# Attention with 16 heads on Trainium2: the softmax division is moved from the probabilities to the attended output

## The chip, the cores and the metric

One core of a Trainium2 chip runs one program. The metric is the device time of the whole program in microseconds (us), lower is better. The engines named below are PE (the matrix engine, with PEld for its weight loads), ACT (scalar engine), DVE (vector engine), POOL (GpSimd), and SP, which issues the DMAs. PSUM has eight banks of 128 x 512 fp32.

## The reference

Two transformer-like blocks follow each other on x of shape (32, 128, 512): 32 sequences of 128 tokens, 512 features. The change touches only the attention of the first block:

```
h   = gamma * layernorm(x) + beta              # gamma, beta from cond, per sequence
qkv = h @ Wqkv.T + bqkv                        # 16 heads of 32
energy = einsum('bhqd,bhkd->bhqk', q, k)
att = softmax(energy, axis=-1) / 512 ** 0.5
out = einsum('bhqk,bhkd->bhqd', att, v)
h1  = out @ Wp.T + bp + x
x1  = gamma * layernorm(h1) + beta + h1
```

The second block (one attention over 512 features, then an MLP of 2048) reads x1.

## The kernel before, in words

The program has three stages. Stage A computes the first block, stage B the attention of the second, stage C its MLP. One tile is one sequence of 128 tokens (t = 0 to 31). Only stage A is changed.

Large products (keys, queries, values, the output projection) are done in fp32r with the operands split into a high and a low half: `split_product` issues three matmuls of 512 columns for each of four slices of the contraction, so each such block has 12 matmuls (lines 547 to 549). Keys and queries are computed for a group of four sequences at a time, one quarter of them in each iteration, a group ahead; so the last four iterations (t = 28 to 31) have none. The normalised input of tile t + 8 is transposed in iteration t (`norm_a`, line 571), so the iterations from t = 24 on have none. Values of tile t + 1 are computed in iteration t; iteration 31 has none.

The order of the matrix engine in an iteration t is written out by hand, and each engine works through its own list in order, waiting on semaphores:

- PE: scores(t) into four banks (32 instructions, line 619), values(t+1), keys, transposes of the probabilities for j = 0 and 1 (`transpose_p`, line 626, four each), queries, transposes for j = 2 and 3, `norm_a(t+8)`, project(t-1), attend(t) (line 637, 32 instructions).
- ACT: `exps(t, j)` for j = 0 to 3 (line 1030): four exponentials each, with the row sums as accumulated output; after j = 1, `round_o(t-1)` (line 1038), which copies the attended output out of its bank; then `copy_k`, and `scale_a` and `round_a` for tile t + 8.
- DVE: the four negated row maxima (line 1290), four reciprocals of the sums (line 1313), `copy_v` (line 1297), `low_o(t-1)` (line 1318), the statistics of two layer norms, four copies of the transposed probabilities (`copy_pt`, line 1308), `norm2`, `copy_q`, `add_x1`, and `residual(t-1)` (line 1328), which reads the projection's bank.
- POOL: the bias of the residual input, `scale_p(t, j)` for j = 0 to 3 (line 1662), which multiplies the 128 x 512 exponentials by the reciprocals, `shift(t-2)`, `norm_a(t+9)`.

So each group of exponentials goes ACT, DVE (reciprocal), POOL (multiplication), PE (transpose). `j` numbers the four banks of scores: bank j holds the heads m * 4 + j. The factor 512 ** -0.5 is applied in `round_o` and `low_o`.

Of the kernel before, what the change touches and what calls it, by code (L numbers as in the profile page):

```python
# [11 lines left out]
P = 128  # L12
# [66 lines left out]
def block_pair_kernel(nc, xt, cond_t, cols_d, bp0_d, bv0_d, pb1_d, b2_d, wg_t, wb_t, wqkv, wp0,  # L79
                      film1, film2, wq1_t, wk1_t, wv1_t, wp1, w1, w2, out):  # L80
    with ExitStack() as ctx:
# [84 lines left out]
        pa = run("pa", [P, HM, C, P])  # L166
        pta = run("pta", [P, HM, C, P])
        o_hi = run("o_hi", [P, 2, C, P], F32R)
# [113 lines left out]
        rec_ready, p_scaled = sem("rec_ready"), sem("p_scaled")  # L282
        o_hi_ready, o_lo_ready = sem("o_hi_ready"), sem("o_lo_ready")
# [58 lines left out]
        def h_full(n):  # L342

            if n < GB:
                return (hf[:, 0], hf[:, 1], pa[:, 2], pa[:, 3])[n]
            return hf[:, n % 2]
# [197 lines left out]
        def _(pe):  # L544
# [78 lines left out]
            def transpose_p(t, j):  # L623
                pe.wait_ge(p_scaled, HM * t + j + 1)
                for m in range(C):
                    last = nc.tensor.transpose(scores_bank[j][:, m * P:(m + 1) * P], pa[:, j, m, :], ident[:])
                last.then_inc(tp_done, 1)

            def attend(t):

                pe.wait_ge(v_copied, t + 1)
                wait(pe, o_lo_ready, t)
                pe.wait_ge(pt_copied, HM * (t + 1))
                for m in range(C):
                    for j in range(HM):
                        f = (m * HM + j) * HD
                        last = nc.tensor.matmul(o_bank[j * HD:(j + 1) * HD, m * P:(m + 1) * P], va[:, t % 2, f:f + HD],
                                                pta[:, j, m, :], start=True, stop=True)
                last.then_inc(pv_done, 1)

# [44 lines left out]
            for t in range(NB):  # L685
                g, b = t // GB, t % GB
                ahead = g + 1 < NG
                scores(t)
                if t + 1 < NB:

                    if t == 0:
                        pe.wait_ge(q_copied, GB)
                    elif (t - 1) // GB + 1 < NG:
                        pe.wait_ge(q_copied, GB + t)
                    else:
                        pe.wait_ge(v_copied, t + 1)
                    values(t + 1)
                if ahead:
                    if b == 0:
                        pe.wait_ge(hi_ready, GB * (g + 2))  # L700
                        pe.wait_ge(lo_ready, GB * (g + 2))

                    if t < 2:
                        pe.wait_ge(k_copied, GB + t)
                    else:
                        pe.wait_ge(h1_ready, t - 1)
                    keys(g + 1, b)
                transpose_p(t, 0)
                transpose_p(t, 1)
                if ahead:  # L710
                    pe.wait_ge(v_copied, t + 2)
                    queries(g + 1, b)
                transpose_p(t, 2)
                transpose_p(t, 3)
                if t + AHEAD < NB:

                    pe.wait_ge(n_scaled_act, t + AHEAD - 2)
                    norm_a(t + AHEAD, x_bank)
                if t > 0:
                    if t == 1:  # L720
                        pe.wait_ge(wa_hi_made, 4)
                        pe.wait_ge(wa_lo_made, 6)

                    if ahead:
                        pe.wait_ge(k_copied, GB + t + 1)
                    else:
                        pe.wait_ge(h1_ready, t - 1)
                    project(t - 1)
                attend(t)


# [43 lines left out]
            pe.wait_ge(n_scaled_act, NB - 2)  # L775
# [198 lines left out]
        def _(act):  # L974
# [49 lines left out]
            def exps(t, j):  # L1024

                act.wait_ge(max_done, HM * t + j + 1)
                wait(act, tp_done, HM * (t - 1) + j + 1)
                for m in range(C):
                    h = j * C + m
                    last = nc.scalar.activation(pa[:, j, m, :], scores_bank[j][:, m * P:(m + 1) * P], ACT.Exp,  # L1030
                                                bias=neg_max[:, j * C + m:j * C + m + 1],
                                                accum_out=sums[:, t % 2, h:h + 1])
                last.then_inc(exp_done, 1)

            def round_o(t):
                act.wait_ge(pv_done, t + 1)
                wait(act, proj_done, t - 1)
                nc.scalar.activation(o_hi[:, t % 2].rearrange("p c t -> p (c t)"), o_bank[:], ACT.Copy, scale=INV_SQRT_D)\
                    .then_inc(o_hi_ready, 1)
# [8 lines left out]
            for t in range(NB):  # L1048
                g, b = t // GB, t % GB
                exps(t, 0)  # L1050
                exps(t, 1)
# [3 lines left out]
                exps(t, 3)  # L1055
                if g + 1 < NG:
                    copy_k(g + 1, b)
                if t + AHEAD < NB:
                    scale_a(t + AHEAD, x_bank)
                    round_a(t + AHEAD)  # L1060
            round_o(NB - 1)
# [133 lines left out]
        def _(dve):  # L1195
# [114 lines left out]
            def recip(t, j):  # L1310

                dve.wait_ge(exp_done, HM * t + j + 1)
                nc.vector.reciprocal(rec[:, j * C:(j + 1) * C], sums[:, t % 2, j * C:(j + 1) * C]).then_inc(rec_ready, 1)  # L1313

            def low_o(t):
                dve.wait_ge(o_hi_ready, t + 1)
                wait(dve, proj_done, t - 1)
                nc.vector.scalar_tensor_tensor(o_lo[:, t % 2].rearrange("p c t -> p (c t)"), o_bank[:], INV_SQRT_D,
                                               o_hi[:, t % 2].rearrange("p c t -> p (c t)").bitcast(F32),
                                               ALU.mult, ALU.subtract).then_inc(o_lo_ready, 1)  # L1320
# [47 lines left out]
            for t in range(NB):  # L1368
# [6 lines left out]
                recip(t, 0)  # L1375
                row_max(t, 3)
                recip(t, 1)
                if t + 1 < NB:
                    copy_v(t + 1)
                if t > 0:  # L1380
                    low_o(t - 1)
                recip(t, 2)
# [12 lines left out]
                recip(t, 3)  # L1395
                copy_pt(t, 0)
# [6 lines left out]
                copy_pt(t, 3)  # L1403
                if t > 1:
# [3 lines left out]

            var_2(NB - 2)
# [207 lines left out]
        def _(pool):  # L1617
# [41 lines left out]
            def scale_p(t, j):  # L1659

                pool.wait_ge(rec_ready, HM * t + j + 1)
                nc.gpsimd.tensor_tensor(pa[:, j], pa[:, j],  # L1662
                                        rec[:, j * C:(j + 1) * C].unsqueeze(2).broadcast_to([P, C, P]), ALU.mult)\
                    .then_inc(p_scaled, 1)

            for t in range(NB):
                add_bias(t, t % 2, xra, bp0, xr_in[t % 2], loaded(t // 2 + 1), xr_ready)
                for j in range(HM):
                    scale_p(t, j)
                if t > 1:  # L1670
                    shift(t - 2)
                if t + AHEAD + 1 < NB:
                    norm_a(t + AHEAD + 1)
# [110 lines left out]
```

## Time and profile before

| | us |
|---|---|
| runs of the kernel before | 1577.86, 1580.72, 1580.98 (median 1580.72) |
| the profiled execution, its time | 1577.86 |
| the profiled execution, its span | 1576.1 |
| first scores of stage A start | 54.8 |
| last attend of stage A ends, about | 547.9 |
| PE, PEld busy over the span | 1531.9 (97%), 1239.2 (79%) |
| DVE, ACT, POOL busy over the span | 780.5 (50%), 596.9 (38%), 578.9 (37%) |

The span runs from the first to the last instruction; the profiled execution took 1.8 us more than its span. A row of a timeline gives the start and the length in us, the engine, the line, the operation, the tiles (written <- read), the number of merged instructions, and in brackets how long the engine had been idle and who released it. Matmuls overlap each other, so the length of a matmul's row is longer than the time for which it keeps the next one off; that time is the distance between two starts.

### The profile page before, as it was taken

The page shows a single profiled execution, that of the slowest core. Times are in us where ns is not written, and L with a number is a line of the kernel's source. Part 1 is how long each engine was busy: PE and PEld are TensorE (multiplying, and loading weights), DVE is VectorE, ACT ScalarE, POOL GpSimd, SP SyncE. Part 2 cuts the span into 40 slices and gives each one's busy share as a digit, 9 for nine tenths or more (in the row PEclk, how much of TensorE's full clock was granted, in tenths as well). Part 3 has the DMA queues.
Part 4 walks back from the last instruction along what each step waited for, and adds up shares of the span by engine and source line. Part 5 has one row for each costly group of instructions (what it writes and reads, how often), then busy time and mean ns, then how long its engine had stood idle before and what let it go on. Part 6 is the DMA issues. An engine that isn't in the chain of part 4 may idle for free. (4 is left out here: it accounts for less than half of the span.)

```text
span 1576.1 us, 25094 instructions
## 1 busy us (share of the span) xinstructions
PE 1531.9 (97%) x8988; PEld 1239.2 (79%) x8988; DVE 780.5 (50%) x1613; ACT 596.9 (38%) x1883; POOL 578.9 (37%) x504
## 2 busy tenths in 40 slices
PE   5999999999998799999999999999999999999999
PEld 3888888888886547777777888888888888888887
DVE  5677777777766645444445524242423324252422
ACT  3655555555534335445556312121211212121210
POOL 5566676767545423444433302121110202121100
PEclk9999999999998899999999999999999999999999
DMA  7122223122214332232224402020100102010100
GB/s 252 55 87 75 94 75 102 68 101 68 75 66 176 128 134 101 102 106 80 80 87 160 154 1 74 7 69 11 67 13 24 55 0 73 7 67 13 53 0 28
DMA packets 56577, 117.72 MB, mean 75 GB/s; under 512 B 6288, under 2 KB 6288, under 8 KB 55984
## 3 DMA queue, kind: packets, MB, share of 16 engines
q1 hardware_dynamic: 56496, 116.65, 21.6%
q8 instruction: 49, 0.80, 0.2%
q14 instruction: 32, 0.26, 0.1%
HBM read 91.33 MB, written 25.30 MB: 74 GB/s over the span
## 5 line engine op out<-in xcount | busy, mean ns | idle before, releaser
L1183 ACT ACTIVATE gf<-bank,cols 128x512 f32<-128x512 f32 x128 | 88.2, 689 | 512.5 <-PE bank L549 512.5
L1599 DVE CAST g_hi<-gf 128x512 fp32r<-128x512 f32 x128 | 68.7, 537 | 427.6 <-ACT gf L1183 427.6
L1030 ACT ACTIVATE pa<-bank,neg_max 128x128 f32<-128x128 f32 x512 | 181.3, 408 | 144.0 <-DVE neg_max L1290 144.0
L547 PE MATMUL bank<-w_hi,g_hi 128*128 128x512 f32 x512 | 200.5, 392 | 0.0
L547 PE MATMUL bank<-hb_hi,w_hi 128*128 128x512 f32 x512 | 199.4, 389 | 0.6 <-issue 0.6
L549 PE MATMUL bank<-w_hi,g_lo 128*128 128x512 f32 x512 | 199.4, 389 | 0.0
L548 PE MATMUL bank<-w_lo,g_hi 128*128 128x512 f32 x512 | 199.2, 389 | 0.0
L549 PE MATMUL bank<-hb_hi,w_lo 128*128 128x512 f32 x512 | 199.2, 389 | 0.0
L548 PE MATMUL bank<-hb_lo,w_hi 128*128 128x512 f32 x512 | 199.2, 389 | 0.0
L1649 POOL TENSOR_TENSOR xrc<-xrc,b 128x512 f32<-128x512 f32 x32 | 48.3, 1536 | 301.8 <-DMA xrc<-x_dram 301.8
L1662 POOL TENSOR_TENSOR pa<-pa,rec 128x512 f32<-128x512 f32 x128 | 132.1, 1040 | 50.8 <-DVE rec L1313 50.8
L1682 POOL TENSOR_TENSOR rstd<-ve,neg_half 128x1 f32<-128x1 f32 x64 | 39.0, 610 | 296.0 <-DVE ve L1420 296.0
L1030 ACT ACTIVATION_READ_ACCUMULATOR pa<-bank,neg_max 128x1 f32 x512 | 127.2, 248 | 0.0
L547 PEld LDWEIGHTS bank<-hb_hi,w_hi 128*128 128x128 f32 x512 | 96.1, 188 | 21.0 <-issue 1.0
L549 PEld LDWEIGHTS bank<-w_hi,g_lo 128*128 128x128 f32 x512 | 96.1, 188 | 20.1
L548 PEld LDWEIGHTS bank<-hb_lo,w_hi 128*128 128x128 f32 x512 | 96.1, 188 | 19.9
L549 PEld LDWEIGHTS bank<-hb_hi,w_lo 128*128 128x128 f32 x512 | 96.1, 188 | 19.9
L548 PEld LDWEIGHTS bank<-w_lo,g_hi 128*128 128x128 f32 x512 | 96.2, 188 | 19.6
L547 PEld LDWEIGHTS bank<-w_hi,g_hi 128*128 128x128 f32 x512 | 96.1, 188 | 19.5
L1685 POOL TENSOR_SCALAR xnb<-xb,rstd 128x512 f32<-128x512 f32 x64 | 104.0, 1625 | 11.8 <-issue 7.0
L1290 DVE TENSOR_REDUCE neg_max<-bank 128x4 f32<-128x512 f32 x128 | 83.6, 679 | 46.3 <-PE bank L619 46.3
L1206 DVE TENSOR_TENSOR g_lo<-gf,g_hi 128x512 fp32r<-128x512 f32 x128 | 96.4, 753 | 4.4
(194 smaller groups left out, 3158.4 us busy)
## 6 DMA issues: line engine op xcount, KB each, us to landing
rows<-st_dram SPq DMA_DIRECT2D x32, 512.0 KB, 4.2
xb<-x_dram SPq DMA_DIRECT2D x64, 256.0 KB, 2.9
xa<-xt_in SPq DMA_DIRECT2D x32, 256.0 KB, 4.4
xra<-xt_in SPq DMA_DIRECT2D x32, 256.0 KB, 2.7
x_dram<-h SPq DMA_DIRECT2D x32, 256.0 KB, 2.0
xrb<-x_dram SPq DMA_DIRECT2D x32, 256.0 KB, 3.6
x_dram<-xrb SPq DMA_DIRECT2D x32, 256.0 KB, 2.0
xrc<-x_dram SPq DMA_DIRECT2D x32, 256.0 KB, 3.6
```

What stands on the lines that cost most here:

```text
L547: nc.tensor.matmul(dst, w_hi, a_hi, start=start, stop=False)
L548: nc.tensor.matmul(dst, w_hi, a_lo, start=False, stop=False)
L549: return nc.tensor.matmul(dst, w_lo, a_hi, start=False, stop=stop)
L1030: last = nc.scalar.activation(pa[:, j, m, :], scores_bank[j][:, m * P:(m + 1) * P], ACT.Exp, bias=neg_max[:, j * C + m:j * C + m + 1], acc ...
L1183: nc.scalar.activation(gf[f % 2][:], bank[f % 2][:], ACT.Gelu, bias=cols[:, B1_COL + f:B1_COL + f + 1])\
L1206: return nc.vector.tensor_tensor(dst, whole, high.bitcast(F32), ALU.subtract)
L1290: nc.vector.tensor_reduce(neg_max[:, j * C:(j + 1) * C], scores_bank[j][:].rearrange("p (h k) -> p h k", h=C), AX.X, ALU.max, negate=True) ...
L1599: nc.vector.tensor_copy(g_hi[:, r, :], gf[f % 2][:]).then_inc(g_hi_ready, 1)
L1649: nc.gpsimd.tensor_tensor(x[:, i], x[:, i], row[:], ALU.add).then_inc(ready, 1)
L1662: nc.gpsimd.tensor_tensor(pa[:, j], pa[:, j], rec[:, j * C:(j + 1) * C].unsqueeze(2).broadcast_to([P, C, P]), ALU.mult)\
L1682: nc.gpsimd.tensor_tensor(rstd1[:, i:i + 1], ve1[:, i:i + 1], neg_half[:, 0:1], ALU.pow).then_inc(rr, 1)
L1685: nc.gpsimd.tensor_scalar(xn[:, slot], x[:, i], rstd1[:, i:i + 1], None, ALU.mult).then_inc(ready, 1)
```

## The change

The exponentials are no longer divided before they are transposed. They go from ACT straight to the transposes, the attended output is multiplied by the reciprocals instead, and POOL's `scale_p` is gone. The attended output lies transposed (features on partitions, queries along the bank), so the reciprocals must be transposed too: DVE takes one reciprocal of all 16 sums, copies it spread over 32 columns a head into `recx` (128 x 512), PE transposes that in four instructions into `x_bank` (`recip_t`), ACT copies it with the factor 512 ** -0.5 into `rs` (`copy_r`), and DVE multiplies the attended output by it into `of` (`scale_o`). `round_o` and `low_o` then read `of`. `pa` has two slots in place of four. PE's order changes: the transposes for j = 0 come before the keys, `norm_a` comes before the transposes for j = 2 and 3, and `recip_t(t-1)` comes after scores(t). ACT's `copy_k` comes before `exps(t, 3)`; POOL's three remaining items are in another order.

```diff
             def transpose_p(t, j):
-                pe.wait_ge(p_scaled, HM * t + j + 1)
+                pe.wait_ge(exp_done, HM * t + j + 1)
                 for m in range(C):
-                    last = nc.tensor.transpose(scores_bank[j][:, m * P:(m + 1) * P], pa[:, j, m, :], ident[:])
+                    last = nc.tensor.transpose(scores_bank[j][:, m * P:(m + 1) * P], pa[:, j % 2, m, :], ident[:])
...
             def attend(t):
                 pe.wait_ge(v_copied, t + 1)
-                wait(pe, o_lo_ready, t)
+                wait(pe, o_scaled, t)
...
+            def recip_t(t):
+                if t + AHEAD < NB:
+                    pe.wait_ge(n_scaled_act, t + AHEAD - 1)
+                else:
+                    pe.wait_ge(r_copied, t)
+                pe.wait_ge(rec_ready, t + 1)
+                flat = recx[:].rearrange("p h d -> p (h d)")
+                for m in range(C):
+                    last = nc.tensor.transpose(x_bank[:, m * P:(m + 1) * P], flat[:, m * P:(m + 1) * P], ident[:])
+                last.then_inc(r_done, 1)
...
                 scores(t)
+                if t > 0:
+                    recip_t(t - 1)
...
                     values(t + 1)
+                transpose_p(t, 0)
...
                     keys(g + 1, b)
-                transpose_p(t, 0)
                 transpose_p(t, 1)
                 if ahead:
                     pe.wait_ge(v_copied, t + 2)
                     queries(g + 1, b)
+                if t + AHEAD < NB:
+                    if t == 0:
+                        pe.wait_ge(n_scaled_act, AHEAD - 2)
+                    else:
+                        pe.wait_ge(r_copied, t)
+                    norm_a(t + AHEAD, x_bank)
                 transpose_p(t, 2)
                 transpose_p(t, 3)
-                if t + AHEAD < NB:
-                    pe.wait_ge(n_scaled_act, t + AHEAD - 2)
-                    norm_a(t + AHEAD, x_bank)
...
+            recip_t(NB - 1)
...
             def exps(t, j):
                 act.wait_ge(max_done, HM * t + j + 1)
-                wait(act, tp_done, HM * (t - 1) + j + 1)
+                wait(act, tp_done, HM * t + j - 1)
...
+            def copy_r(t):
+                act.wait_ge(r_done, t + 1)
+                wait(act, o_scaled, t)
+                nc.scalar.activation(rs[:], x_bank[:], ACT.Copy, scale=INV_SQRT_D).then_inc(r_copied, 1)
+
             def round_o(t):
-                act.wait_ge(pv_done, t + 1)
+                act.wait_ge(o_scaled, t + 1)
                 wait(act, proj_done, t - 1)
-                nc.scalar.activation(o_hi[:, t % 2].rearrange("p c t -> p (c t)"), o_bank[:], ACT.Copy, scale=INV_SQRT_D)\
-                    .then_inc(o_hi_ready, 1)
+                nc.scalar.activation(o_hi[:, t % 2], of[:], ACT.Identity).then_inc(o_hi_ready, 1)
...
                 exps(t, 0)
+                if t > 0:
+                    copy_r(t - 1)
                 exps(t, 1)
                 if t > 0:
                     round_o(t - 1)
                 exps(t, 2)
-                exps(t, 3)
                 if g + 1 < NG:
                     copy_k(g + 1, b)
+                exps(t, 3)
...
+            copy_r(NB - 1)
             round_o(NB - 1)
...
-            def recip(t, j):
-                dve.wait_ge(exp_done, HM * t + j + 1)
-                nc.vector.reciprocal(rec[:, j * C:(j + 1) * C], sums[:, t % 2, j * C:(j + 1) * C]).then_inc(rec_ready, 1)
+            def recip(t):
+                wait(dve, r_done, t)
+                dve.wait_ge(exp_done, HM * (t + 1))
+                nc.vector.reciprocal(rec[:], sums[:, t % 2, :]).then_inc(rec_made, 1)
+                dve.wait_ge(rec_made, t + 1)
+                nc.vector.tensor_copy(recx[:], rec[:].unsqueeze(2).broadcast_to([P, HEADS, HD]))\
+                    .then_inc(rec_ready, 1)
+
+            def scale_o(t):
+                dve.wait_ge(r_copied, t + 1)
+                wait(dve, o_lo_ready, t)
+                dve.wait_ge(pv_done, t + 1)
+                nc.vector.tensor_tensor(of[:].rearrange("p c t -> p (c t)"), o_bank[:], rs[:], ALU.mult)\
+                    .then_inc(o_scaled, 1)
 
             def low_o(t):
                 dve.wait_ge(o_hi_ready, t + 1)
                 wait(dve, proj_done, t - 1)
-                nc.vector.scalar_tensor_tensor(...)
+                low_half(o_lo[:, t % 2], of[:], o_hi[:, t % 2]).then_inc(o_lo_ready, 1)
...
-                recip(t, 0)
                 row_max(t, 3)
-                recip(t, 1)
                 if t + 1 < NB:
                     copy_v(t + 1)
+                copy_pt(t, 0)
                 if t > 0:
-                    low_o(t - 1)
-                recip(t, 2)
+                    scale_o(t - 1)
...
-                recip(t, 3)
-                copy_pt(t, 0)
+                if t > 0:
+                    low_o(t - 1)
                 copy_pt(t, 1)
...
                 copy_pt(t, 3)
+                recip(t)
...
+            scale_o(NB - 1)
...
-            def scale_p(t, j):
-                pool.wait_ge(rec_ready, HM * t + j + 1)
-                nc.gpsimd.tensor_tensor(pa[:, j], pa[:, j],
-                                        rec[:, j * C:(j + 1) * C].unsqueeze(2).broadcast_to([P, C, P]), ALU.mult)\
-                    .then_inc(p_scaled, 1)
-
             for t in range(NB):
-                add_bias(t, t % 2, xra, bp0, xr_in[t % 2], loaded(t // 2 + 1), xr_ready)
-                for j in range(HM):
-                    scale_p(t, j)
+                if t + AHEAD + 1 < NB:
+                    norm_a(t + AHEAD + 1)
                 if t > 1:
                     shift(t - 2)
-                if t + AHEAD + 1 < NB:
-                    norm_a(t + AHEAD + 1)
+                add_bias(t, t % 2, xra, bp0, xr_in[t % 2], loaded(t // 2 + 1), xr_ready)
```

In the first group of tiles `h_full` uses `of` and `rs` in place of two slots of `pa`, and a later transpose into `x_bank` waits for the last `copy_r`. Stages B and C are unchanged.

## Rows read from the trace of the kernel before

**Rows 1.** The page: busy time, share of the span, instructions by engine.

```profile
PE 1531.9 (97%) x8988; PEld 1239.2 (79%) x8988; DVE 780.5 (50%) x1613; ACT 596.9 (38%) x1883; POOL 578.9 (37%) x504
```

**Rows 2.** Windows: length, each engine's busy us and count, clock, DMA, GB/s.

```profile
200.00:300.00 100.00, 100.00 (x832) 82.80 (x831) 75.20 (x164) 56.94 (x246) 69.55 (x60) 1.00 0.24 80
...
486.00:502.20 16.20, 13.26 (x116) 9.80 (x106) 9.78 (x20) 6.18 (x33) 7.19 (x7) 0.79 0.90 324
502.20:517.10 14.90, 11.75 (x108) 8.79 (x104) 9.77 (x20) 6.18 (x33) 7.20 (x7) 0.89 0.22 73
517.10:533.00 15.90, 12.96 (x108) 9.70 (x104) 9.78 (x20) 6.18 (x33) 7.18 (x7) 0.79 0.20 68
533.00:547.90 14.90, 9.89 (x96) 7.35 (x92) 9.44 (x20) 6.17 (x33) 7.16 (x7) 0.77 0.65 230
```

**Rows 3.** Timeline of PE, iteration t = 2: first instruction of each block.

```profile
83.90 1.17 PE L619 MATMUL bank<-ka,qa 32*128 32x128 f32 x32
85.00 0.50 PE L547 MATMUL bank<-wv_hi,h_hi 128*128 128x512 f32 x1
...
87.89 0.39 PE L547 MATMUL bank<-h_hi,wk_hi 128*128 128x512 f32 x1
...
90.62 1.03 PE L626 MATMUL bank<-ident,pa 128*128 128x128 f32 x8
91.41 0.48 PE L547 MATMUL bank<-h_hi,wq_hi 128*128 128x512 f32 x1
...
94.25 1.03 PE L626 MATMUL bank<-ident,pa 128*128 128x128 f32 x8
...
99.43 1.17 PE L619 MATMUL bank<-ka,qa 32*128 32x128 f32 x32
```

**Rows 4.** Timeline of PE: scores of t = 23, 24 and 25.

```profile
410.33 1.17 PE L619 MATMUL bank<-ka,qa 32*128 32x128 f32 x32
...
425.86 1.17 PE L619 MATMUL bank<-ka,qa 32*128 32x128 f32 x32
...
440.92 1.17 PE L619 MATMUL bank<-ka,qa 32*128 32x128 f32 x32
```

**Rows 5.** Timeline of PE ahead of the loop: four transposes between two product blocks.

```profile
45.54 0.60 PE L571 MATMUL bank<-ident,xa 128*128 128x128 f32 x4
45.90 0.48 PE L547 MATMUL bank<-h_hi,wk_hi 128*128 128x512 f32 x1
```

**Rows 6.** Waits, 55 to 550 us: total us, times, longest.

```profile
DVE h L1328 <- PE bank L549: 46.9, 31, 2.8
...
PE bank L626 <- POOL pa L1662: 14.0, 16, 3.7
```

**Rows 7.** Groups by line: busy us, mean ns of one, idle time before.

```profile
L1328 DVE TENSOR_TENSOR h<-bank,xra 128x512 f32<-128x512 f32 x32 | 22.1, 692 | 47.6 <-PE bank L549 47.6
```

**Rows 8.** Timelines of PE, DVE and ACT, iteration t = 13.

```profile
255.00 1.17 PE L619 MATMUL bank<-ka,qa 32*128 32x128 f32 x32
...
256.24 1.29 DVE L1290 TENSOR_REDUCE neg_max<-bank 128x4 f32<-128x512 f32 x2 [1.45 <-PE bank L619]
...
256.96 0.37 ACT L1030 ACTIVATE pa<-bank,neg_max 128x128 f32<-128x128 f32 x1 [3.42 <-DVE neg_max L1290]
...
259.72 0.64 ACT L1038 ACTIVATE o_hi<-bank 128x512 fp32r<-128x512 f32 x1
260.20 0.41 ACT L1030 ACTIVATE pa<-bank,neg_max 128x128 f32<-128x128 f32 x1
...
262.94 0.78 ACT L1022 ACTIVATE ka<-bank,cols 128x512 f32<-128x512 f32 x1
```

**Rows 9.** Timeline of PE, iteration t = 29, without keys and queries.

```profile
502.19 1.17 PE L619 MATMUL bank<-ka,qa 32*128 32x128 f32 x32
...
511.73 1.12 PE L626 MATMUL bank<-ident,pa 128*128 128x128 f32 x4 [0.45 <-POOL pa L1662]
512.49 0.78 PE L547 MATMUL bank<-wp_hi,o_hi 128*128 128x512 f32 x1
```

More of the change, by code:

```diff
@@ L165, in block_pair_kernel @@
         pa_at = run.offset
-        pa = run("pa", [P, HM, C, P])
+        pa = run("pa", [P, 2, C, P])
         pta = run("pta", [P, HM, C, P])
+        recx = run("recx", [P, HEADS, HD])
+        rs = run("rs", [P, D])
+        of = run("of", [P, C, P])
         o_hi = run("o_hi", [P, 2, C, P], F32R)
@@ L281, in block_pair_kernel @@
         tp_done, pt_copied, pv_done = sem("tp_done"), sem("pt_copied"), sem("pv_done")
-        rec_ready, p_scaled = sem("rec_ready"), sem("p_scaled")
-        o_hi_ready, o_lo_ready = sem("o_hi_ready"), sem("o_lo_ready")
+        rec_made, rec_ready, r_done, r_copied = sem("rec_made"), sem("rec_ready"), sem("r_done"), sem("r_copied")
+        o_scaled, o_hi_ready, o_lo_ready = sem("o_scaled"), sem("o_hi_ready"), sem("o_lo_ready")
         proj_done, xr_ready, h1_ready = sem("proj_done"), sem("xr_ready"), sem("h1_ready")
@@ L344, in h_full @@
             if n < GB:
-                return (hf[:, 0], hf[:, 1], pa[:, 2], pa[:, 3])[n]
+                return (hf[:, 0], hf[:, 1], of[:], rs[:].rearrange("p (c t) -> p c t", c=C))[n]
             return hf[:, n % 2]
@@ L774, in _ @@
             pe.wait_ge(film_copied, 2)
-            pe.wait_ge(n_scaled_act, NB - 2)
+            pe.wait_ge(r_copied, NB)
             for c in range(C):
@@ L1026, in exps @@
                 act.wait_ge(max_done, HM * t + j + 1)
-                wait(act, tp_done, HM * (t - 1) + j + 1)
+                wait(act, tp_done, HM * t + j - 1)
                 for m in range(C):
-                    h = j * C + m
-                    last = nc.scalar.activation(pa[:, j, m, :], scores_bank[j][:, m * P:(m + 1) * P], ACT.Exp,
+                    h = m * HM + j
+                    last = nc.scalar.activation(pa[:, j % 2, m, :], scores_bank[j][:, m * P:(m + 1) * P], ACT.Exp,
                                                 bias=neg_max[:, j * C + m:j * C + m + 1],
@@ L1317, in low_o @@
                 wait(dve, proj_done, t - 1)
-                nc.vector.scalar_tensor_tensor(o_lo[:, t % 2].rearrange("p c t -> p (c t)"), o_bank[:], INV_SQRT_D,
-                                               o_hi[:, t % 2].rearrange("p c t -> p (c t)").bitcast(F32),
-                                               ALU.mult, ALU.subtract).then_inc(o_lo_ready, 1)
+                low_half(o_lo[:, t % 2], of[:], o_hi[:, t % 2]).then_inc(o_lo_ready, 1)
             def residual(t):
```

## Prediction, on record before the change was run

> **What bounds the kernel now.** I read four views in this order: the page's busy shares, windows over stage A, PE's timeline inside one iteration, and the waits.
>
> The page has PE at 97% of the span and nothing else above 50% [rows 1]. Since a matmul's row is longer than the time it keeps its successor off, this alone doesn't prove that PE is the limit. The windows tell the stages of the loop apart. Between 200 and 300 us PE is busy 100.00 of 100 us at clock 1.00, while DVE has 75, POOL 70 and ACT 57 [rows 2]. In the last four iterations PE is busy 13.26 of 16.2, 11.75 of 14.9, 12.96 of 15.9 and 9.89 of 14.9, and the mean clock is 0.77 to 0.89, so part of each runs at 1.2 GHz and not at 2.4 [rows 2]: there a chain through the other engines sets the pace. The proof that PE is the limit in the first 28 is in the periods. Iteration 23 takes 425.86 - 410.33 = 15.53 us, as does t = 2 (99.43 - 83.90), and iteration 24, which differs for PE by four missing transposes, takes 440.92 - 425.86 = 15.06 [rows 3, 4]. Take work from PE and the iteration shrinks by 0.47 us at once; work added there should lengthen it. PE waits for POOL only where keys and queries are missing: the 16 waits sum to 14.0 us [rows 6], four blocks of transposes in each of four iterations.
>
> So `scale_p`, the work removed, blocks PE in 4 of 32 iterations, and the work added to PE lies in all of them.
>
> **The change, part by part.** The sum is made for the profiled execution, 1577.86 us (span 1576.1 plus 1.8); the median of the runs shown is 1580.72, 2.9 above it.
>
> *Removed.* POOL loses four multiplications an iteration and DVE four small reciprocals. In the loop's first 28 iterations nothing on PE waits for them, so this is worth nothing there.
>
> *`recip_t` on PE.* Four transposes in iterations 1 to 27. The price as a distance between starts has two bounds. Ahead of the loop, four lone transposes take 45.90 - 45.54 = 0.36 us until the next product starts [rows 5]. Values take 87.89 - 85.00 = 2.89 us when they follow scores, queries 94.25 - 91.41 = 2.84 when they follow transposes, keys 90.62 - 87.89 = 2.73 when they follow another product [rows 3]; with `recip_t` in between, values follow transposes and take 0.05 less. That gives 0.31 as the lower bound. The upper is the 0.47 by which iteration 23 exceeds 24. I take the middle, 0.39; times 27 that is 10.5 us.
>
> *The moved transposes.* A run of eight is split: values, four, keys, four, queries. Now eight take 91.41 - 90.62 = 0.79 and the queries behind them 0.11 more than keys behind values: 0.90. Split, it is 2 x (0.36 + 0.11) = 0.94. That is 0.04 more; the rows are rounded to 0.01, so between 0.02 and 0.06, and 28 x 0.03 = 0.8 us. `norm_a` stays in a run of twelve transposes: nothing.
>
> *Does anything make PE wait in these iterations?* Time 0 is the start of scores; distances between starts are from [rows 8] and [rows 3]. PE: scores to 1.1, `recip_t` to 1.5, values to 4.3, j = 0 to 4.7, keys to 7.5, j = 1 to 7.9, queries to 10.7, norm to 11.1, j = 2 to 11.5, j = 3 to 11.9, project to 14.8, attend to 15.9. DVE's first maximum starts 256.24 - 255.00 = 1.24 after the scores' start, which is 0.14 after their end, and two maxima last 1.29, so 0.6 each; ACT's first exponential starts at 1.96. A group of four exponentials takes (259.72 - 256.96) / 2 = 1.38, `round_o` 0.48 (260.20 - 259.72), `copy_k` 0.78; `copy_r`, also a 128 x 512 ACT copy out of PSUM, gets `round_o`'s 0.48. So exps 0 ends at 3.3, `copy_r` at 3.8, exps 1 at 5.2. `scale_o` is the step with a new wait. It stands behind `copy_v` (values end at 4.3, released 0.14 later like the maxima) and `copy_pt(0)`; with the 0.6 of a maximum for each it starts at 5.7 and, at the 0.69 of the nearest row (a DVE product-bank read with an SBUF operand [rows 7]), ends at 6.4. `round_o` ends at 6.9, exps 2 at 8.3, `copy_k` at 9.1, exps 3 at 10.5 to 10.7. PE wants it at 11.5. Slack: 0.8 us. Behind ACT's wait for `scale_o` stand exps 2 and 3, and for them wait the transposes for j = 2 and 3, `copy_pt` and attend, so this is the chain that matters. `low_o` ends near 8.6 and project needs it at 11.9. The last `copy_pt` ends near 12.9 and attend needs it at 14.8. The reciprocal and its spread copy have no row of their size; nothing at the least, at the most 0.69 each [rows 7], they end by 14.3; `recip_t` wants them at 17.0. `residual` waits for project until 15 anyway: DVE has waited there 46.9 us in 31 times, 1.5 each [rows 6]. POOL's list is shorter by four 128 x 512 multiplications. SP's loads and stores wait for the same events, in the same order. I cost all of this at nothing; the cover is PE itself, and where it goes by d us in every iteration, the price is 28 d.
>
> *The last four iterations.* Now j = 3 starts at 511.73 - 502.19 = 9.54 after the scores and project at 10.3 [rows 9]. In the new order values end at 4.3, `scale_o` at 6.4, `round_o` at 6.9, exps 2 at 8.3, exps 3 at 9.7, so j = 3 starts near 9.8. What lay between exps 3 and j = 3 (9.54 - 1.96 - 4 x 1.38 - 0.48 = 1.6) is gone, but `copy_r` (0.48) and the wait for `scale_o` (ACT finished exps 1 at 5.2 and stands until 6.4) take its place. That is 0.25 later in each of three iterations, 0.8 us. Iteration 31 has no values, so `copy_pt(0)` and `scale_o` come earlier: exps 3 ends near 8.7, against 9.54 now: 0.8 us less. `recip_t(31)` adds 0.4. Together +0.4. The time at 1.2 GHz will be about what it is, since the idle time ahead of project is: now 9.54 less 4.0 of scores and values and 1.1 of three transposes, 4.4 us; then 0.6, 2.7 and 1.0, 4.3 us. Its bounds are the two rivals on these four below.
>
> Sum: 10.5 + 0.8 + 0.4 = 11.7 us, 1577.9 + 11.7 = 1589.6 for an execution like the profiled one and 1592.4 for one at the median. I say 1591.
>
> PE's busy share leaves a question. The Trainium skill (Perfetto Trace Analysis, "Identifying the Most-Contended Engine") calls matmul busy time a bad measure of headroom and wants the weight-load share read. That share is 82.80 of 100 us here [rows 2], which would leave 17 us in 100, and the new transposes would cost nothing: 1579. The periods of iterations 23 and 24 speak against it.
>
> The Trainium skill (TensorE: Matmul & The Clock Gate, "Part 4: PE-mode transpose") has about 275 ns for a transpose in a kernel. Taken as a price that makes an estimate of 1.1 us for four, 34 us for 31 times, and 1612. The row of eight here lasts 1.03 us but holds the queries off for 0.79 [rows 3], so durations overlap and the distance counts.
>
> **The rivals.**
>
> *A stall behind `scale_o`.* If DVE reaches `scale_o` or finishes it over 0.8 us later than I reckon, j = 3 starts late in every iteration. For it: DVE exchanges four small operations for a spread copy and a product of 128 x 512, and ACT now waits in the middle of its exponentials. Against it: each step has a row. At 0.5 us late in 28 iterations it adds 14: 1605. It decides from 0.8 us of slip.
>
> *The last four iterations gain.* If the clock stays full there, they take 9.8 + 0.4 + 2.9 + 1.0 = 14.1 three times and 13.0 once, 55.7 with `recip_t(31)`, against 61.9 in the windows [rows 2]: 6.2 less, so 11.3 - 6.2 = 5.1 in total, 1583 or 1586 at the median. For it: `values`, `recip_t` and j = 0 now run without a break. Against it: PE still idles about 4 us before project.
>
> *PE has room.* The transposes hide in gaps between matmuls. Then nothing moves by more than 1 us: 1580. Against it: the 0.47 us.
>
> *Faster: the POOL hop was the whole limit of the last four.* If they ran at PE's own length, about 10 us each, 61.9 would fall to 40 and the total by 22 - 11.3 = 11: 1567 to 1570. It decides when these four give back more than 11.3, 2.8 each. Against it: sixteen exponentials take 5.5 us from 1.96 on, and project and attend (4) stand behind them, which no order here shortens below 11.5.
>
> **How the numbers follow.** Forecast 66% (1587 to 1596), stall 13% (to 1610), gain in the last four 12%, PE has room 5%, faster 4%. The range 1584 to 1602 leaves out the last two and most of the deep stall. A difference of 0.2%, about 3 us, is what a measurement of this kernel tells from none. The forecast, the stall and the gain are slower by more; of the rest about 6% lies within it: slower 0.90, within 0.06, faster 0.04.
>
> **What would show it.** Right: scores of full iterations 15.9 to 16.0 us apart, PE still busy 100 of 100; the four transposes of `recx` hold the values off by 0.36 to 0.44; no wait of PE behind exponentials before t = 28; the last four together within 2 us of 61.9. Wrong: PE idle before j = 2 or 3 in the full iterations, with `scale_o` at its root; or the four transposes costing under 0.2; or a clock of 1.00 in the last four.

## The result and the profile after

The changed kernel takes 1592.88 us (median of 4 runs, 1591.71 to 1594.01), the kernel before 1579.29 in the same series (4 runs, 1577.75 to 1580.98). The ratio is 1.0086, with a 95% interval of 1.0068 to 1.0103: slower by 0.9%. The profiled execution took 1592.22 us with a span of 1590.4, 14.3 more than the span before; the forecast was 11.7 more.

The page of the changed kernel, busy time by engine, answers to [rows 1]:

```profile
PE 1544.8 (97%) x9116; PEld 1250.8 (79%) x9116; DVE 829.0 (52%) x1581; ACT 616.8 (39%) x1915; POOL 461.1 (29%) x376
```

POOL gave up 118 us of work, PE gained 128 instructions, DVE 49 us. The span went with PE. PE's share is 97% as before, and the windows show why that is no sign of standing still. They answer to [rows 2]; the last window is a piece of iteration 31.

```profile
200.00:300.00 100.00, 100.00 (x838) 82.48 (x838) 85.16 (x155) 60.58 (x256) 43.32 (x32) 1.00 0.24 80
...
547.00:557.20 10.20, 7.50 (x24) 5.63 (x25) 7.03 (x14) 5.34 (x27) 3.44 (x3) 0.51 0.55 220
```

In the middle of the loop PE is busy 100.00 of 100 us, as it was, while POOL fell from 70 to 43 us and DVE rose from 75 to 85. The second window matters further down: in 10.2 us of the last iteration the clock was almost all the time 1.2 GHz (0.51 of full).

One full iteration (t = 12) on PE, first instruction of each group, answers to [rows 3]:

```profile
242.21 1.17 PE L622 MATMUL bank<-ka,qa 32*128 32x128 f32 x32
243.31 0.66 PE L653 MATMUL bank<-ident,recx 128*128 128x128 f32 x4
243.72 0.47 PE L550 MATMUL bank<-wv_hi,h_hi 128*128 128x512 f32 x1
...
246.58 0.60 PE L629 MATMUL bank<-ident,pa 128*128 128x128 f32 x4
246.93 0.48 PE L550 MATMUL bank<-h_hi,wk_hi 128*128 128x512 f32 x1
...
249.79 0.60 PE L629 MATMUL bank<-ident,pa 128*128 128x128 f32 x4
250.14 0.48 PE L550 MATMUL bank<-h_hi,wq_hi 128*128 128x512 f32 x1
...
252.98 0.60 PE L574 MATMUL bank<-ident,xa 128*128 128x128 f32 x4
253.42 1.04 PE L629 MATMUL bank<-ident,pa 128*128 128x128 f32 x8
254.21 0.48 PE L550 MATMUL bank<-wp_hi,o_hi 128*128 128x512 f32 x1
...
257.16 1.08 PE L640 MATMUL bank<-pta,va 128*32 128x128 f32 x32
258.17 0.39 PE L622 MATMUL bank<-ka,qa 32*128 32x128 f32 x4
```

The reader should see that no row has an idle time in brackets, and that the starts follow the forecast's list: scores to 1.1, `recip_t` to 1.5, values to 4.4, the end at 258.17 - 242.21 = 15.96 us. The four transposes of `recx` keep the values off by 243.72 - 243.31 = 0.41 us; the values then take 2.86 and not 2.89. Every full iteration from the third on takes 15.96 us (it was 15.53, once 15.77), and the four without `norm_a` take 15.48 to 15.49 (15.06 to 15.08).

The differences between starts on PE, put together by stretch. `B and C` runs from the first product with `g_hi_b` to the end of the span.

| stretch | before | after | difference | forecast |
|---|---|---|---|---|
| ahead of the first scores | 54.76 | 52.77 | -2.0 | 0 |
| iterations 0 to 27 | 431.40 | 442.90 | +11.5 | +11.3 |
| iterations 28 to 31, with `recip_t(31)` | 61.75 | 64.22 | +2.5 | +0.4 |
| from there to the first `g_hi_b` | 43.46 | 43.72 | +0.3 | 0 |
| B and C | 984.73 | 986.79 | +2.1 | 0 |

The last line belongs to code that the change leaves alone, and the first to code in which it only changes two buffers. Over all twelve profiled executions in this study the first lies between 52.4 and 54.8 us and the last between 984.6 and 988.6, and the executions with the old and the new stage A overlap in both. So both differences are of the size by which executions of the same code differ, and that they cancel here is luck. The forecast's total was 2.6 short, most of it in the last four iterations; how much of that belongs to the change is worked out further down.

### The profile page after: what moved, and what is told of

It is laid out like the page before. It is cut to its first block, busy times and chain, and to the rows that moved or that the text cites. A ratio compares the mean times of both kernels' runs of the same rounds, so it can differ in the third digit from the quotient of the medians.

```text
span 1590.4 us, 25350 instructions
## 1 busy us (share of the span) xinstructions
PE 1544.8 (97%) x9116; PEld 1250.8 (79%) x9116; DVE 829.0 (52%) x1581; ACT 616.8 (39%) x1915; POOL 461.1 (29%) x376
## 4 chain that ended last, share of the span: by engine, by line
PE 90%; DMA 3%; DVE 2%; ACT 2%; issue 1%; POOL 1%; SPq 1%; DVEq 0%; ACTq 0%
PE bank L550 25%; PE bank L552 25%; PE bank L551 25%; PE bank L629 3%; PE bank L622 2%; PE bank L640 2%; DMA xb<-x_dram 2%; PE bank L904 1%; PE bank L653 1%; DMA x_dram<-xrb 1%; PE bank L773 1%; PE bank L762 1%; PE bank L815 1%; PE bank L574 1%; ACT pa L1052 1%
## 5 line engine op out<-in xcount | busy, mean ns | idle before, releaser
L1712 POOL TENSOR_TENSOR rstd<-ve,neg_half 128x1 f32<-128x1 f32 x64 | 39.0, 610 | 295.8 <-DVE ve L1459 295.8
L1052 ACT ACTIVATION_READ_ACCUMULATOR pa<-bank,neg_max 128x1 f32 x512 | 113.0, 221 | 0.0
L1676 POOL TENSOR_TENSOR rstd<-ve,neg_half 128x1 f32<-128x1 f32 x32 | 33.5, 1047 | 227.7 <-DVE ve L1259 227.7
```

The lines of the kernel that those rows point to most:

```text
L1052: last = nc.scalar.activation(pa[:, j % 2, m, :], scores_bank[j][:, m * P:(m + 1) * P], ACT.Exp, bias=neg_max[:, j * C + m:j * C + m + 1], ...
L1712: nc.gpsimd.tensor_tensor(rstd1[:, i:i + 1], ve1[:, i:i + 1], neg_half[:, 0:1], ALU.pow).then_inc(rr, 1)
```

## The experiments

The spans below are those of the profiled execution, to be set against 1576.1 (before) and 1590.4 (after). The period is the distance between two starts of scores in full iterations.

**e1: one transpose in place of four.**

```diff
             def recip_t(t):
...
-                for m in range(C):
+                for m in range(1):
```

> The changed kernel, with one transpose in place of four in recip_t, so that only a quarter of the reciprocals is refreshed (the division is left incomplete). If the loss of the full iterations is PE's own time, and a transpose in a row costs about 0.1 us between starts, the scores of full iterations lie 15.96 - 3 x 0.1 = 15.66 to 15.69 us apart, and the span falls by about 31 x 0.29 = 9 us, to 1581 to 1583. If the loss came from the new chain through DVE and ACT (copy, copy_r, scale_o), nothing of that is changed and the period stays at 15.96.

Period 15.64, span 1578.5 (1580.3 us, one run). Three transposes less take 15.96 - 15.64 = 0.32 us off each iteration, 0.107 each, though the copy, `copy_r` and `scale_o` are all still there. PE's own time it is. The price of one transpose was set a little low: the period came out 0.02 under the range given, and the span 2.5.

**e2: eight transposes.**

```diff
             def recip_t(t):
...
-                for m in range(C):
+                for m in list(range(C)) * 2:
```

> The changed kernel, with recip_t's four transposes issued twice. PE's own time: the period rises by four more in a row, 8 take 0.79 to 0.87 where 4 take 0.36, so 16.39 to 16.45 us, and the span rises by about 12 to 15 us to 1602 to 1605. Chain through DVE and ACT: copy_r waits for it, but ACT reaches copy_r 1.4 us later than it needs, so the period stays at 15.96. A price by the length of one row of 0.27 us for each transpose would give 17.05.

Period 16.38, span 1604.5 (1606.32 us, one run): 0.42 more for four, 0.105 each. The period is 0.01 under the range given, the span within it. One, four and eight transposes lie on a line. Where it starts, with no transpose at all, was not run in this kernel; e6, further down, comes nearest. The price by the length of a row, 0.27 us each, is refuted.

**e3: the kernel before, with four transposes that nobody reads.**

```diff
                 scores(t)
+                if t > 0:
+                    pe.wait_ge(n_scaled_act, min(t - 1 + AHEAD, NB - 1) - 1)
+                    for m in range(C):
+                        nc.tensor.transpose(x_bank[:, m * P:(m + 1) * P], ident[:], ident[:])
                 if t + 1 < NB:
```

> The kernel before, with four transposes of the identity into the free bank after the scores of iterations 1 to 31, whose results nobody reads; its arithmetic is otherwise whole. PE's own time: the period of full iterations rises from 15.53 by 0.39 to 0.43 to 15.92 to 15.96, and iterations 1 to 27 give 11 us, the ratio to before is about 1.007. If the reordering and the new work on DVE and ACT bear most of the changed kernel's loss, the period stays under 15.7 and the ratio under 1.004.

Ratio 1.0056, interval 1.0037 to 1.0075 (1588.01 us, median of 4 runs); period 15.88. So four transposes on PE, with POOL, DVE and ACT as they were, bring 0.35 of the 0.43 us. That is the middle of the forecast's two bounds (0.31 and 0.47) less 0.04, and a little under what I expected of this run; the ratio's interval holds 1.007 as well. What is left, 0.08, asks for e6.

**e4: the transposes for j = 0 back behind the keys.** The rival of a stall behind `scale_o` never showed in the changed kernel. This run takes its cover away.

```diff
                     values(t + 1)
-                transpose_p(t, 0)
                 if ahead:
                     ...
                     keys(g + 1, b)
+                transpose_p(t, 0)
                 transpose_p(t, 1)
```

> The changed kernel, with the transposes for j = 0 back behind the keys, beside those for j = 1. By the chain of the prediction copy_pt(0) then starts at 7.6 after the scores in place of 5.1, scale_o ends at 8.9, round_o at 9.4, exps 2 at 10.8, copy_k at 11.6, exps 3 at 13.0, and the transposes for j = 3 wait for that at 13.1 where PE is ready at 11.1 to 11.5: a stall of 1.6 to 2 us in each full iteration, period 17.5 to 17.9, span 1635 to 1645. The rival, that the order of the transposes is of no account, gives 15.92 to 15.96 and a span of 1589 to 1591.

Period 17.43, span 1632.1 (1633.9 us, one run). The chain of the prediction holds link by link. PE, DVE and ACT in the iteration that starts at 259.34:

```profile
259.34 1.17 PE L622 MATMUL bank<-ka,qa 32*128 32x128 f32 x32
...
266.40 1.03 PE L629 MATMUL bank<-ident,pa 128*128 128x128 f32 x8
...
272.42 0.66 PE L629 MATMUL bank<-ident,pa 128*128 128x128 f32 x4 [1.32 <-ACT pa L1052]
```

```profile
267.04 0.69 DVE L1338 COPY pta<-bank 128x512 f32<-128x512 f32 x1 [2.47 <-PE bank L629]
267.65 0.68 DVE L1353 TENSOR_TENSOR of<-bank,rs 128x512 f32<-128x512 f32 x1
```

```profile
268.36 0.63 ACT L1066 ACTIVATE o_hi<-of 128x512 fp32r<-128x512 f32 x1 [3.66 <-DVE of L1353]
```

`copy_pt(0)` starts at 7.70 after the scores (expected 7.6), `scale_o` starts at 8.31, `round_o` at 9.02, and j = 3 at 272.42 - 259.34 = 13.08 (expected 13.1). PE stands for 1.32 us in front of it, and the iteration grows by 17.43 - 15.96 = 1.47. That is a little less than expected: the stall was to be 1.6 to 2, the period 17.5 at least and the span 1635. The early place of j = 0 is therefore what keeps the new chain under PE's work; it is not a matter of taste. Here a stall moves every iteration by its full length once its cover is gone.

**e5: the kernel before without `scale_p`.**

```diff
             def transpose_p(t, j):
-                pe.wait_ge(p_scaled, HM * t + j + 1)
+                pe.wait_ge(exp_done, HM * t + j + 1)
...
-                for j in range(HM):
-                    scale_p(t, j)
```

> The kernel before without scale_p: the probabilities are never divided, and PE's transposes wait for the exponentials; nothing is put in its place. It tells what POOL's work cost by itself. Forecast: nothing in the full iterations (period 15.53), and in each of the last four j = 3 starts 1.4 us sooner (8.1 after the scores and not 9.5), so these take 55 to 57 us in place of 61.9 and the span falls by 5 to 7, to 1569 to 1572. The rival, that POOL's multiplications slow the full iterations too (through the ports that it shares or through later transposes), gives a period of 15.4 or less and a span under 1566.

Period 15.53, span 1572.0 (1573.78 us, one run). What the change takes from POOL is worth nothing in a full iteration, to the hundredth of a us. The last four took 57.78 us, 4.0 less, where 5 to 7 were expected. The transposes for j = 3 start 8.2 us after the scores there, nearly as expected (8.1), but project then takes 4.0 to 5.4 us and not 2.95 as in the full iteration shown above, at a granted clock of 0.76 to 0.88: the time at 1.2 GHz was not reckoned with.

**e6: e5 with the changed kernel's order on PE.**

```diff
                     values(t + 1)
+                transpose_p(t, 0)
...
-                transpose_p(t, 0)
                 transpose_p(t, 1)
...
+                if t + AHEAD < NB:
+                    pe.wait_ge(n_scaled_act, t + AHEAD - 2)
+                    norm_a(t + AHEAD, x_bank)
                 transpose_p(t, 2)
                 transpose_p(t, 3)
-                if t + AHEAD < NB:
-                    ...
```

> The kernel e5_no_scale_p with the changed kernel's order on PE alone: the transposes for j = 0 between values and keys, norm_a ahead of the transposes for j = 2 and 3. The probabilities are not divided either. It prices the order. The four transposes of the identity cost 0.35 us and the whole change 0.43, so 0.08 should be the order: period 15.61, where the forecast had 0.03. If it stays at 15.53 to 15.56, the 0.08 belongs to recip_t's own operands or waits.

Period 15.59, span 1568.6 (1570.43 us, one run). The order costs 0.06 us an iteration, between the forecast's 0.03 and the 0.08 of the remainder; 0.35 + 0.06 leaves 0.02 of the 0.43 without a place. Beside e1, which has this order and one transpose (15.64), the first transpose costs 0.05, less than each of the next three (0.107); DVE and ACT differ between the two runs as well, so this is no clean price. And this run shows something else. From t = 28 on, e5 and e6 issue the same instructions in the same order. Their last four iterations, by windows, e5 first:

```profile
485.30:499.20 13.90, 11.62 (x108) 9.00 (x104) 9.76 (x20) 6.18 (x33) 3.12 (x3) 0.88 0.96 325
499.20:514.60 15.40, 13.09 (x109) 9.86 (x106) 9.77 (x20) 6.18 (x33) 3.09 (x3) 0.78 0.31 118
514.60:528.70 14.10, 11.81 (x108) 8.99 (x104) 9.76 (x20) 6.18 (x33) 3.12 (x3) 0.88 0.22 75
528.70:543.10 14.40, 9.99 (x97) 7.36 (x93) 9.46 (x20) 6.17 (x33) 3.09 (x3) 0.76 0.67 229
```

```profile
485.60:498.20 12.60, 10.30 (x111) 7.88 (x107) 9.28 (x20) 6.20 (x33) 3.15 (x3) 1.00 0.93 316
498.20:510.80 12.60, 10.26 (x112) 7.90 (x108) 9.71 (x21) 6.19 (x33) 3.11 (x3) 1.00 0.44 166
510.80:524.80 14.00, 11.70 (x108) 9.06 (x104) 10.12 (x21) 6.20 (x33) 3.12 (x3) 0.88 0.29 95
524.80:538.70 13.90, 9.75 (x96) 7.31 (x92) 9.44 (x20) 6.19 (x33) 3.10 (x3) 0.75 0.62 226
```

The columns are the window, its length, the busy time of PE, PEld, DVE, ACT and POOL, the granted clock, the DMA share and GB/s. At clock 1.00 an iteration takes 12.6 us, at 0.88 13.9 to 14.1, at 0.78 15.4. Between the two runs PE starts its transposes at the same places after the scores, to 0.02 us in iteration 28, and the four iterations together differ by 4.7 us with the clock. Why it fell sooner in e5 is open. For the question of e5 this means that POOL's work cost the last four 4.0 us by one execution and 8.7 by the other (61.75 - 53.1).

**e7: the kernel before with project moved forward in the last four iterations.** The hole that the change was not able to close lies in front of project, and project's inputs are ready in the middle of it.

```diff
                 if ahead:
                     pe.wait_ge(v_copied, t + 2)
                     queries(g + 1, b)
+                else:
+                    pe.wait_ge(h1_ready, t - 1)
+                    project(t - 1)
                 transpose_p(t, 2)
                 transpose_p(t, 3)
...
-                if t > 0:
+                if t > 0 and ahead:
...
```

> The kernel before, whole, with one move on PE: in the last four iterations project(t-1) goes between the transposes for j = 1 and those for j = 2, where PE waits for POOL. low_o ends 6.3 us after the scores, so project runs from 6.7 to 9.6 and the transposes for j = 2 and 3 find their inputs ready: attend starts near 11.4, the iteration takes 12.4 us and not 14.9 to 16.0, and the last four give back 10 to 12 us: ratio 0.993 to 0.994. If the chain through the exponentials were the bound whatever PE does in it, the gain would be under 3 us, ratio over 0.998.

Ratio 0.9967, interval 0.9955 to 0.9978 (1573.13 us, median of 6): faster, but about half of what was expected. Iteration 28 took 12.60 us, the next 16.45. PE and POOL in that one:

```profile
505.35 0.66 PE L626 MATMUL bank<-ident,pa 128*128 128x128 f32 x4 [3.50 <-POOL pa L1662]
```

```profile
503.03 1.27 POOL L1649 TENSOR_TENSOR xra<-xra,bp 128x512 f32<-128x512 f32 x1 [6.35 <-DMA xra<-xt_in]
504.25 4.03 POOL L1662 TENSOR_TENSOR pa<-pa,rec 128x512 f32<-128x512 f32 x4
```

PE waits for POOL's multiplications, these stand behind the bias in POOL's list, and the bias waits for x. Its load is issued once `residual` has freed the buffer (at 498.1 here), while the 4 MB of raw weights still fill the queues, and lands 4.9 us later. With a shorter iteration the load comes too late, and an addition that nobody needs yet holds up the one that everybody waits for.

**e8: the same move in the changed kernel.**

> The changed kernel with the same move of project. low_o ends 8.0 us after the scores there, since scale_o and round_o stand before it, so project runs from 8.1 to 11.0, attend starts near 12.8 and an iteration takes 13.8: the last four give back 7 to 9 us of 63.7, ratio to the kernel before 1.002 to 1.005. It stays slower, because the 0.43 us of each full iteration (11.5 us) is more than that. If the last four of both kernels are then alike, the ratio is 1.001 or less.

Ratio 1.0087, interval 1.0072 to 1.0103 (1591.26 us, median of 6, 1587.10 to 1595.18), outside what was expected. In the profiled execution (span 1587.6) the last four with `recip_t(31)` took 59.31 us and not 64.22, so the move gave back 4.9 there, not 7 to 9: iterations 28 and 29 took 14.1 us (13.8 expected), 30 took 15.7. The median is only 1.6 us under that of the changed kernel in another series, and the ratio is no better than the changed kernel's 1.0086. The runs spread over 8 us, and they part by the mean granted clock: the three at 0.995 to 0.997, the profiled one among them, took 1587.10 to 1590.18, the three at 0.991 to 0.992 took 1592.33 to 1595.18. All runs of the changed kernel lie at 0.990 to 0.992. So part of the 4.9 may be the clock of the one execution that was profiled; what the move itself is worth here stays open.

**e9: e7, and POOL adds the bias last.**

```diff
             for t in range(NB):
-                add_bias(t, t % 2, xra, bp0, xr_in[t % 2], loaded(t // 2 + 1), xr_ready)
                 for j in range(HM):
                     scale_p(t, j)
                 if t > 1:
                     shift(t - 2)
                 if t + AHEAD + 1 < NB:
                     norm_a(t + AHEAD + 1)
+                add_bias(t, t % 2, xra, bp0, xr_in[t % 2], loaded(t // 2 + 1), xr_ready)
```

> The kernel e7_before_project_early (the kernel before with project moved in the last four iterations) with one more edit: POOL adds the bias of the residual input after scale_p, shift and norm_a and not ahead of them. In e7 PE stood 3.5, 1.9 and 5.0 us in iterations 29 to 31 behind POOL's multiplications, and these behind the bias, which waited for a load of x. If that is the cause, all four take 12.4 to 12.6, 50 to 51 us in place of 57.0, and the ratio to the kernel before is 0.992 to 0.993. If something else held PE (the granted clock, the copies on DVE), the last four stay over 55 and the ratio at 0.9965.

Ratio 0.9935, interval 0.9921 to 0.9948 (1568.12 us, median of 5 runs, 1566.78 to 1569.06): just above the range given, 10 us faster than the kernel before, 25 faster than the changed one in its series. Iterations 28 to 30 take 12.60, 12.58 and 12.61. The last takes 15.4 and not 12.5, so the four take 53.2 and not 50 to 51:

```profile
526.56 0.66 PE L626 MATMUL bank<-ident,pa 128*128 128x128 f32 x4 [3.68 <-POOL pa L1662]
527.96 1.11 PE L626 MATMUL bank<-ident,pa 128*128 128x128 f32 x4 [0.74 <-POOL pa L1662]
...
533.99 1.06 PE L626 MATMUL bank<-ident,pa 128*128 128x128 f32 x8
```

It has no values to fill the 3.7 us before the first transposes; after that idle time the transposes last 1.11 us and not 0.66, and project takes until 534. What held PE in e7 is thus shown, and it was 3.8 us of 57.0.

**e10: the kernel before with that POOL order alone.**

> The kernel before with that second edit alone, project where it was. There the reciprocal of the first group ends 0.1 to 0.3 us before POOL is through with the bias, so the transposes start at most 0.3 sooner in each of the last four, and the load of x has landed in time. Forecast: no change, ratio 0.999 to 1.001, last four 60 to 62 us. If POOL's order is worth something by itself, e9's gain shows here too and the ratio is under 0.997.

Ratio 1.0002, interval 0.9992 to 1.0011 (1578.45 us, median of 10). The last four took 62.94 us, 0.9 above the range given, though the transposes for j = 3 start at the same place (9.52 us after the scores, 9.53 before). By itself the order of POOL's list is worth nothing: a wait counts only once somebody is behind it.

## Why the prediction was right, point by point

- *The number.* 1591 was forecast and 1592.88 measured. The 1591 holds a base of 1579.3, which happens to be the median measured for the kernel before, so the miss of 1.9 lies in the difference: 11.7 forecast, 13.6 between the medians, 14.3 between the profiled executions.
- *PE is the limit of the first 28 iterations.* Right. Take-away (e5) gives nothing, four idle transposes (e3) give most of the loss, and the price follows the number of transposes (e1, e2). The Trainium skill (Perfetto Trace Analysis, "Identifying the Most-Contended Engine") would read 17 us of headroom from a weight-load share of 82.80 of 100 us. The share in the same window is 82.48 now, and the transposes added still lengthened the period (by 0.35 us for four in e3, 0.42 for four more in e2); here the measured periods decide against that reading.
- *`recip_t`: 0.39 an iteration.* e3 measures 0.35 for four transposes there, within the bounds 0.31 and 0.47. In the changed kernel the order's part comes on top.
- *The moved transposes: 0.03.* e6 measures 0.06. The forecast priced the run that was split and let `norm_a` change its place for nothing; which of the two has the other 0.03 was not measured. The two terms together were 0.42 by forecast and are 0.43.
- *Nothing makes PE wait.* Right. From the second iteration to the 28th no row of PE has an idle time before it. A row of DVE and two of ACT from the iteration shown above:

```profile
247.98 0.68 DVE L1353 TENSOR_TENSOR of<-bank,rs 128x512 f32<-128x512 f32 x1
```

```profile
248.70 0.63 ACT L1066 ACTIVATE o_hi<-of 128x512 fp32r<-128x512 f32 x1 [1.14 <-DVE of L1353]
...
252.20 0.41 ACT L1052 ACTIVATE pa<-bank,neg_max 128x128 f32<-128x128 f32 x1
```

  `scale_o` starts at 247.98 - 242.21 = 5.77 after the scores (forecast 5.7). ACT does stand in the middle of its exponentials, 1.14 us, as foreseen. The last exponential starts at 9.99 after the scores and ends, accumulator read included, at 10.5; PE wants it at 11.6. The spread copy, bounded by 0 and 0.69, takes 0.51 on average.
- *The last four: +0.4, measured +2.5.* This is the term that was mis-sized, and the sign given for it failed by a little: the four were to lie within 2 us of 61.9 and took 64.22. Four profiled executions, three of them with the chain of the kernel before, show how much of the 2.5 is the change:

| execution | j = 3 starts after the scores, t = 28 to 31 | from there to attend, sum of the four |
|---|---|---|
| before | 9.53, 9.54, 9.53, 9.53 | 19.58 |
| e3 | 9.53, 9.53, 9.53, 9.52 | 18.66 |
| e10 | 9.52, 9.52, 9.52, 9.52 | 20.81 |
| changed | 9.94, 9.96, 9.95, 9.43 | 20.40 |

  The starts of j = 3 add up to 1.15 us more than before, where the forecast had 0.8 - 0.8 = 0, and `recip_t(31)` takes 0.49 where it had 0.4: 1.6 for the change in place of 0.4. Iterations 28 to 30 carry 0.5 of the excess (9.95 and not 9.8), iteration 31 carries 0.7 (9.43 and not 8.7). The other 0.8 lies behind j = 3, in which project runs partly at 1.2 GHz. That stretch differs by 2.2 us between executions in which j = 3 starts at the same place, so the 0.8 cannot be told from chance. By the forecast the time at 1.2 GHz would stay about what it is. It did: by the granted clocks of the four iterations (0.79, 0.89, 0.79, 0.77 before; 0.89, 0.80, 0.89, 0.69 after) my estimate, twice the missing share of the clock times the length of the iteration, is 23.6 us before and 23.7 after. It only lies elsewhere. Iteration 31 after, then before:

```profile
543.57 1.17 PE L622 MATMUL bank<-ka,qa 32*128 32x128 f32 x32
...
547.10 1.07 PE L629 MATMUL bank<-ident,pa 128*128 128x128 f32 x4 [1.76 <-ACT pa L1052]
...
553.00 1.12 PE L629 MATMUL bank<-ident,pa 128*128 128x128 f32 x4 [0.28 <-ACT pa L1052]
553.77 0.78 PE L550 MATMUL bank<-wp_hi,o_hi 128*128 128x512 f32 x1
...
558.39 1.08 PE L640 MATMUL bank<-pta,va 128*32 128x128 f32 x32
```

```profile
533.02 1.17 PE L619 MATMUL bank<-ka,qa 32*128 32x128 f32 x32
...
543.31 0.78 PE L547 MATMUL bank<-wp_hi,o_hi 128*128 128x512 f32 x1
...
546.90 1.08 PE L637 MATMUL bank<-pta,va 128*32 128x128 f32 x32
```

  PE has no values there, stands 1.76 us, and from 547.0 to 557.2 the clock is at 1.2 GHz almost throughout. The four transposes for j = 0 last 1.07 us and not 0.66, so `copy_pt(0)` and `scale_o` come later: `scale_o` starts 5.25 us after the scores, 0.5 sooner than in iteration 30, where the forecast had the end of the chain 1.1 sooner. Project takes 558.39 - 553.77 = 4.62 us here, 3.59 in the same iteration before and 2.95 in a full one. That the clock alone can make such differences is shown by e5 against e6; how much of the late j = 3 of iteration 31 it explains was argued from the rows and not tested.
- *The rivals.* The stall behind `scale_o` did not come, with about 1 us to spare, and e4 shows its price. The gain in the last four did not come in the changed kernel. "PE has room" is refuted by e3. "POOL's hop was the whole limit of the last four" is refuted by e5 and e6: without it they lose 4.0 or 8.7 us of 61.75, not 22. The chain through sixteen exponentials stays, and it is the place of project in the order that lets PE work under it (e9).

## What to carry to other kernels

Where an engine is full, ask of a change only what it puts on that engine: four instructions of 0.1 us in 27 iterations outweigh 118 us of work taken from an engine that PE waits for only in the last four. Price small instructions by the distance between starts, and look for two iterations that differ by just that instruction; here that gave the upper bound of the price. Where a chain through other engines sets the pace, look for work that is ready and can be moved into the hole (e7, e9) before you shorten the chain, and then look at who now stands behind a wait that used to be harmless. Where the clock moves within a stretch, one profiled execution is not enough to size a change of 1 us: the last four took 60.8 to 62.9 us in three executions with the same chain.

## What the runs showed of the hardware that was not expected

The granted clock makes the same matmuls of an iteration, with the same idle time on PE, take 12.6, 13.9 or 15.4 us (e5 and e6), at 1.00, 0.88 and 0.78. Every fall to 1.2 GHz in the rows of the last four iterations came after PE had stood, but standing does not settle it. In iteration 28 of both e5 and e6 PE stands 0.3, 1.2 and 0.7 us in front of the transposes; those for j = 3 then last 1.12 us in e5 and 0.65 in e6. In e4 PE stands 1.32 us in every full iteration, and between 200 and 300 us the granted clock is 1.00.

`add_x1`, a DVE operation with two SBUF inputs, lasts 1774 ns in the median in the changed kernel (740 at least), where the median was 743 before. Its arithmetic is the same. It now runs while POOL adds the bias, which also has two SBUF inputs, as here at 256.00 and 255.75:

```profile
256.00 1.78 DVE L1393 SCALAR_TENSOR_TENSOR h<-nb,rstd,h 128x512 f32<-128x512 f32 x1
```

```profile
255.75 1.47 POOL L1688 TENSOR_TENSOR xra<-xra,bp 128x512 f32<-128x512 f32 x1
```

`residual` then starts at 257.70 without a wait, where DVE had waited 1.5 us for project on average; PE does not wait for it, so the period shows nothing of this. That POOL is the cause was not tested alone, but the kept executions agree on it. Between 80 and 430 us, in the five that have the changed kernel's order on POOL (the changed kernel, e1, e2, e4, e8), `add_x1` overlaps the bias and lasts 1.75 to 1.78 us every time but one, and that one, in e1, is without the overlap and lasts 0.74. In the other seven it overlaps the bias once each in e9 and e10, at 0.95, and otherwise, mostly beside `norm_a` on POOL, lasts 0.74 to 1.13. By the Trainium skill (GPSIMD Engine Reference, "Key points"), POOL shares its SBUF interfaces with VectorE and contends with DVE operations that have two SBUF inputs; the rows agree with that.
